# A two-layer block in one program: ScalarE takes the first layer norm of the dispatch stage, VectorE finds six of eight inverse roots from bits, and TensorE's order in a group is rearranged

## The reference, cut to what matters

```python
x = layernorm(x + attn(x))      # x: (4, 1024, 128) float32; attn ends in silu(y) @ W_out
x = layernorm(x + ffn(x))
# ffn: logits = flat @ router_w.T ; the 2 best of 8 experts, weights from a softmax
#      out  = sum over chosen experts e of mlp_e(flat) * weight + mlp_shared(flat)
#      mlp(x) = square(relu(x @ w_fc.T)) @ w_proj.T       d_ff = 512
# layernorm(x) = (x - mean) / sqrt(var + 1e-5), over the 128 features
```

## Time and profile before

| | |
|---|---|
| median of 3 runs | 514.8 us (514.63 to 515.39) |
| the profiled execution | 513.47 us; its span from first to last instruction is 511.6 us |
| TensorE busy in the span | 450.6 us (88%) |
| VectorE busy | 374.9 us (73%) |
| ScalarE busy | 357.7 us (70%) |
| GpSimd busy | 294.5 us (58%) |
| mean granted TensorE clock | 0.967 of full |

### The profile page before, as it was taken

One profiled execution on the slowest core, in us unless ns is written; L12 is line 12 of the kernel. 1 busy time (PEld: TensorE's weight loads), 2 busy tenths in 40 slices (PEclk: granted clock), 3 DMA queues, 4 the chain that ended last, 5 costly groups with the idle time before them and its releaser, 6 DMA issues.

```text
span 511.6 us, 7508 instructions
## 1 busy us (share of the span) xinstructions
PE 450.6 (88%) x2162; PEld 293.2 (57%) x2162; DVE 374.9 (73%) x863; ACT 357.7 (70%) x545; POOL 294.5 (58%) x250
## 2 busy tenths in 40 slices
PE   8757899998999988887888999689999999999391
PEld 5313344433443333344666777479999999999340
DVE  6776999998999999999998976533433334555075
ACT  3839799998999999971555566427666666566256
POOL 3235567777677787873767677714455555655200
PEclk9979999999999999999799999979999999999897
DMA  8010010109955566000111111131222221221373
GB/s 264 4 43 0 1 43 1 44 2 375 350 210 209 211 222 229 32 1 2 45 42 49 36 49 57 54 90 52 68 69 78 65 64 57 70 57 54 102 279 113
DMA packets 39448, 48.55 MB, mean 95 GB/s; under 512 B 5408, under 2 KB 25058, under 8 KB 38896
## 3 DMA queue, kind: packets, MB, share of 16 engines
q1 hardware_dynamic: 34048, 39.06, 22.7%
q0 software_dynamic: 5216, 8.70, 5.5%
q10 hardware_dynamic: 144, 0.31, 0.2%
HBM read 19.17 MB, written 29.11 MB: 94 GB/s over the span
## 4 chain that ended last, share of the span: by engine, by line
DVE 41%; PE 35%; ACT 8%; issue 7%; POOL 4%; DMA 3%; DVEq 0%; ACTq 0%; POOLq 0%; SPq 0%
PE routed_ph L1388 13%; PE routed_po L1401 12%; DVE memory_y_raw L735 10%; DVE memory_prod L726 10%; DVE memory_feat L711 4%; PE dispatch_spo L927 3%; POOL table_scratch L1080 3%; ACT finish_xo L1566 2%; PE memory_nsum L585 2%; DVE dispatch_xrow L1148 2%; PE dispatch_sph L917 2%; PE routed_px L1376 1%; DVE memory_query L706 1%; DMA memory_feat<-memory_last_rows 1%; ACT memory_feat L377 1%
## 5 line engine op out<-in xcount | busy, mean ns | idle before, releaser
L465 POOL TENSOR_TENSOR memory_feat<-memory_feat,memory_p_tok 128x1024 f32<-128x1024 f32 x64 | 121.5, 1920 | 54.7 <-ACT memory_feat L377 54.7
L585 PE MATMUL memory_nsum<-memory_feat,tri 128*128 128x512 f32 x256 | 116.5, 598 | 10.8 <-ACT memory_last_rows L386 4.3
L1364 POOL DMA_INDIRECT pick_scratch<-routed_ob,routed_xg x71 | 70.9, 998 | 74.3 <-DVE routed_ob L1485 60.8
L585 PEld LDWEIGHTS memory_nsum<-memory_feat,tri 128*128 128x128 f32 x256 | 46.9, 190 | 70.0 <-issue 66.7
L1080 POOL DMA_INDIRECT table_scratch<-dispatch_xrow,dispatch_slot x64 | 61.8, 966 | 27.7 <-issue 17.1
L1434 ACT ACTIVATE routed_rel<-routed_ph 128x512 f32<-128x512 f32 x71 | 42.3, 597 | 46.1 <-PE routed_ph L1388 46.1
L1388 PE MATMUL routed_ph<-routed_xs,routed_w1c 128*128 128x256 f32 (+1 forms) x368 | 71.3, 337 | 0.9 <-DVE routed_w2c L1471 0.9
L1485 DVE TENSOR_SCALAR routed_ob<-routed_po,routed_xg 128x128 f32<-128x128 f32 x71 | 22.6, 348 | 67.2 <-PE routed_po L1401 67.2
L1401 PE MATMUL routed_po<-routed_w2c,routed_hid 128*128 128x128 f32 x568 | 71.1, 275 | 0.5 <-ACT routed_hid L1443 0.5
L726 DVE TENSOR_TENSOR memory_prod<-memory_nsum,memory_query 128x1024 f32<-128x1024 f32 x58 | 68.2, 1215 | 1.9 <-PE memory_nsum L585 1.9
L1401 PEld LDWEIGHTS routed_po<-routed_w2c,routed_hid 128*128 128x128 f32 x568 | 67.0, 192 | 0.8 <-ACT routed_hid L1443 0.7
(11 more groups left out here) (187 smaller groups left out, 662.1 us busy)
## 6 DMA issues: line engine op xcount, KB each, us to landing
table_scratch<-memory_blank SPq DMA_DIRECT2D x68, 260.0 KB, 2.8
finish_pick<-pick_scratch SPq DMA_DIRECT2D x16, 256.0 KB, 5.6
routed_xg<-table_scratch SPq DMA_DIRECT2D x25, 130.0 KB, 2.2
x_tok<-x SPq DMA_DIRECT2D x4, 512.0 KB, 3.9
w<-w_up SPq DMA_DIRECT2D x2, 1024.0 KB, 9.0
w<-w_down SPq DMA_DIRECT2D x2, 1024.0 KB, 11.1
out<-finish_xo SPq DMA_DIRECT2D x8, 256.0 KB, 2.3
routed_xg<-table_scratch SPq DMA_DIRECT2D x21, 65.0 KB, 1.9
```

The lines of the kernel that those rows point to most:

```text
L465: last = nc.gpsimd.tensor_tensor(v, v, pv, ALU.mult)
L585: last = nc.tensor.matmul(nsum[:, o:o + 512], tri[:], feat[:, i % U, h, q * 512:(q + 1) * 512], start=True, stop=True)
L1364: nc.gpsimd.indirect_dma_start(out=pick_dram, in_=ob[:, u, h, :], in_offset=None, out_offset=bass.IndirectOffsetOnAxis(ap=xg[:, t % XU, h, ...
```

## The change

ScalarE does `normalise` as an Identity activation with a scale (the root) and a bias (`shift` = -mean times root, one more VectorE instruction). The root is found in `invert_root`: GpSimd's power for groups 0 and 1 alone, else from bits with three Newton steps. `res`, `scale`, `shift` are double buffered. In TensorE's loop `project` goes ahead of `turn_x`, `turn_x` behind `up(g, 0)`, `route` behind the first `down`, and `rank` or `total` behind the third `down`. ScalarE's list gets `normalise` in four places, and `keep_x` and `slope` move.

```diff
-POWERS = (0, 1, 2, 4, 6)
+POWERS = (0, 1)
+STEPS = 3
...
                 for g in range(1, NG):
-                    if g + 1 < NG:
-                        turn_x(g + 1)
                     if g + 2 < NG:
                         project(g + 2)
                     up(g, 0)
                     if g + 1 < NG:
+                        turn_x(g + 1)
+                    down(g - 1, 0)
+                    if g + 1 < NG:
                         route(g + 1)
-                    down(g - 1, 0)
                     up(g, 1)
                     down(g - 1, 1)
+                    up(g, 2)
+                    down(g - 1, 2)
                     if g + 1 < NG:
                         rank(g + 1)
                     else:
                         total()
-                    up(g, 2)
-                    down(g - 1, 2)
                     up(g, 3)
...
+            def normalise(g):
+                act.wait_ge(shift_done, g + 1)
+                for t in range(GT):
+                    last = nc.scalar.activation(xrow[:, 0, g * GT + t, 0:D], res[:, g % 2, t, :], ACT.Identity,
+                                                bias=shift[:, g % 2, t:t + 1], scale=scale[:, g % 2, t:t + 1])
+                last.then_inc(x1_done, 1)
...
                 if i == NT - 3:
+                    normalise(0)
                     for g in range(2, NG - 2):
                         silu(g)
                     nc.scalar.copy(tri_r[:], tri[:])
...
                 keep_x(0)
                 second_row(0)
                 slope(0)
+                normalise(1)
                 keep_y(2)
                 for g in range(NG):
-                    if 0 < g < NG - 1:
-                        keep_x(g + 1)
                     relu(g, 0)
                     square(g, 0)
                     if 0 < g < NG - 1:
+                        keep_x(g + 1)
                         second_row(g + 1)
                     relu(g, 1)
...
                     square(g, 1)
                     if g == 0:
                         second_row(1)
-                    if 0 < g < NG - 1:
-                        slope(g + 1)
+                    if g + 2 < NG:
+                        normalise(g + 2)
                     relu(g, 2)
                     square(g, 2)
-                    if g == 0:
-                        slope(1)
+                    if g < NG - 1:
+                        slope(g + 1)
...
-            def normalise(g):
+            def invert_root(g):
                 dve.wait_ge(var_done, g + 1)
+                if g >= 2:
+                    dve.wait_ge(x1_done, g - 1)
...
-                for n in range(1 if g in POWERS else 4):
+                steps = 1 if g in POWERS else STEPS
+                for n in range(steps):
...
-                for t in range(GT):
-                    last = nc.vector.tensor_scalar(xrow[:, 0, g * GT + t, 0:D], res[:, t, :], mv[:, t, 0:1],
-                                                   root[:, t:t + 1], ALU.subtract, ALU.mult)
-                last.then_inc(x1_done, 1)
+                nc.vector.scalar_tensor_tensor(shift[:, g % 2], mv[:, :, 0], -1.0, scale[:, g % 2], ALU.mult, ALU.mult
+                                               ).then_inc(shift_done, 1)
...
                     if g + 2 < NG:
                         residual(g + 2)
+                        invert_root(g + 2)
                     if g + 1 < NG:
                         choose(g + 1)
-                    if g + 2 < NG:
-                        normalise(g + 2)
```

More of the change, by code:

```diff
@@ L177, in __init__ @@
         self.newton = sb("newton", [P, 2, GT])
+        self.scale = sb("scale", [P, 2, GT])
+        self.shift = sb("shift", [P, 2, GT])
         self.off = sb("off", [P, E])
@@ L790, in dispatch @@
         stride, base0, past, owner, moved = early.stride, early.base0, early.past, early.owner, early.moved
-        bits = early.bits
+        bits, scale, shift = early.bits, early.scale, early.shift
         ones_r = sb("ones_r", [P, P], F32R)
@@ L813, in dispatch @@
         root_done = sem("root_done")
+        shift_done = sem("shift_done")
         x1_done = sem("x1_done")
@@ L1121, in residual @@
                 dve.wait_ge(proj_done, g + 1)
-                if g:
-                    dve.wait_ge(x1_done, g)
-                else:
+                if g >= 2:
+                    dve.wait_ge(x1_done, g - 1)
+                elif g == 0:
                     dve.wait_ge(mem.x_tok_in, 16 * B)
-                link(nc.vector.tensor_tensor(res[:].rearrange("p t c -> p (t c)"), pb[:],
+                link(nc.vector.tensor_tensor(res[:, g % 2].rearrange("p t c -> p (t c)"), pb[:],
                                              x_tok[:, group(g), :].rearrange("p t c -> p (t c)"), ALU.add))
                 for t in range(GT):
-                    last = nc.vector.bn_stats(stats[:, t, :], res[:, t, :])
+                    last = nc.vector.bn_stats(stats[:, t, :], res[:, g % 2, t, :])
                 link(last)
@@ L1142, in normalise @@
                     link(nc.vector.tensor_scalar(root[:].bitcast(I32), bits[:], -1.0, float(ROOT_SEED), ALU.mult, ALU.add))
-                for n in range(1 if g in POWERS else 4):
+                steps = 1 if g in POWERS else STEPS
+                for n in range(steps):
                     link(nc.vector.tensor_tensor(newton[:, 0], var[:], root[:], ALU.mult))
                     link(nc.vector.scalar_tensor_tensor(newton[:, 1], newton[:, 0], -0.5, root[:], ALU.mult, ALU.mult))
-                    link(nc.vector.scalar_tensor_tensor(root[:], newton[:, 1], 1.5, root[:], ALU.add, ALU.mult))
-                for t in range(GT):
-                    last = nc.vector.tensor_scalar(xrow[:, 0, g * GT + t, 0:D], res[:, t, :], mv[:, t, 0:1],
-                                                   root[:, t:t + 1], ALU.subtract, ALU.mult)
-                last.then_inc(x1_done, 1)
+                    link(nc.vector.scalar_tensor_tensor(root[:] if n + 1 < steps else scale[:, g % 2], newton[:, 1], 1.5,
+                                                        root[:], ALU.add, ALU.mult))
+                nc.vector.scalar_tensor_tensor(shift[:, g % 2], mv[:, :, 0], -1.0, scale[:, g % 2], ALU.mult, ALU.mult
+                                               ).then_inc(shift_done, 1)
             def choose(g):
@@ L1243, in tail @@
                 elif i == NT - 3:
-                    normalise(0)
+                    invert_root(0)
                 elif i == NT - 2:
@@ L1252, in rest @@
                 count(0)
-                normalise(1)
+                invert_root(1)
                 reduce(NT - 4)
```

4 lines of the change are left out of this document (3 added, 1 removed).

## The result

The changed kernel takes 529.6 us (median of 6 runs, 528.84 to 531.38), the kernel before in the same session 514.7 us (6 runs, 513.16 to 515.39): ratio 1.030, 95% interval 1.0276 to 1.0327. The change makes the kernel 3% slower. The direction was as predicted; 525.4 us and the range up to 528.0 were too low.

A forecast was written before the change was run, and what follows sets the result against it. TensorE's start of the first routed `up` was taken to bound the kernel; opening 7.3, loop 2.0, `total` 1.75, `down(7)` -0.5 sum to +10.6 us, 514.8 to 525.4 us, 8-in-10 range 519.5 to 528.

The forecast's parts named there:

- the half clock: TensorE's opening at 1.2 GHz: `project` 1.7, `route` 1.55, first half of the sums 2.7 for 1.8 us.
- the collision of `scale` with the next VectorE instruction: GpSimd's `scale` beside x1: moving x1 saves 1.4 us of VectorE time in two groups, left as slack.
- TensorE's own work in a group: Loop: one full group counted at 10.15 us from start to start.
- What bounds the kernel: Routed stage untouched; the first routed `up`, at 341.44, decides, and the end follows when TensorE reaches `total`.
- First stop: Opening: `normalise(0)` ahead of `keep_y(1)` on ScalarE; `project(1)` +3.2 us, `place(0)` +4.6 us.
- Second stop: Opening: `normalise(1)` ahead of `keep_y(2)` on ScalarE; `project(2)` +7.1 us, `up(1, 0)` +7.3 us.
- the third stop: `normalise(2)` ahead of `keep_y(3)` on ScalarE, which ends at 262.1; mentioned but not priced apart.
- The loop: From `up(1, 0)` to `up(7, 0)`: exposed hand-overs `keep_y` and `keep_x` make it 67.1 us for 65.1, +2.0.
- That VectorE's gain is slack: Loop: VectorE comes down to some 8.1 us a group, under TensorE's 10.15; the roots change nothing.
- The end: `total` moves behind an `up` and a `down`, +1.75 us; `down(7)` taken at 5.7 us, -0.5.
- Sum: All terms together +10.6 us; the median 514.8 becomes 525.4 us.
- Rival 4: Newton steps run into GpSimd's `scale`, or half clock returns in each group; up to +14 us, 528.8; chance 0.07.

The follow-up runs named there:

- e3: Changed kernel with `normalise(0)` moved behind `keep_y(1)` and `normalise(1)` behind `keep_y(2)`: 552.0 us, ratio 1.017, on a slower chip.
- e6: e12 with TensorE's loop order, the early ranks and total, and ScalarE's `keep_x` back as before, VectorE's order left as changed: 532.7 us, ratio 1.038.
- e12: The same kernel as e3, run again beside a steadier kernel before: 524.6 us, ratio 1.019.
- e14: e12 with `normalise(g+2)` behind `keep_y(g+3)`, `choose` ahead of the root, `total` at its old place, `keep_x` ahead of `relu(g, 0)`: 520.5 us, ratio 1.010.
- e5: The changed kernel run again without any edit: 530.3 us, ratio 1.030.
- e7: Kernel before with only the roots of groups 2 to 7 from bits, three Newton steps, no power on GpSimd for them: 515.4 us, ratio 1.003.
- e11: Changed kernel with one edit, `choose(g+1)` ahead of the root of group g+2 on VectorE: 550.4 us, ratio 1.071.
- e9: Changed kernel with `total()` alone back at its old place, ahead of `up(7, 2)` and `down(6, 2)`: 527.5 us, ratio 1.026.
- e13: Changed kernel with products whose values are overwritten, ten, twelve and eight ahead of `project(1)`, `project(2)`, `project(3)`: 528.0 us, ratio 1.027.
- e10: e6 with VectorE's order of before restored as well (residual, choose, root): 528.8 us, ratio 1.030.
- e17: Kernel before with `add_shared(6)` between the table's halves, group 6's root from bits, four unused products behind `down(7)`: 511.6 us, ratio 0.994.
- e8: Kernel before with one edit, `add_shared(6)` between the two halves of VectorE's table of tiles: 514.8 us, ratio 1.002.

## Why the prediction was right in direction and too low

The way and the path were right; the size was not. The steps that failed are three terms of the sum: the half clock (charged to 5 us of work at the first stop, it lasted some 10; with what followed from it 2.4 us in the opening, 0.5 in group 1 and 0.8 at the end), the collision of `scale` with the next VectorE instruction (put at nothing, 1.5 us), and TensorE's own work in a group (10.15 us for 10.55, 1.0 over the loop).

- **What bounds the kernel** held: the routed stage did not move, and the start of its first `up` carries the whole difference.
- **First stop**: said +4.6 at `place(0)`, measured 6.2 (249.53 less the 1.3 of the memory stage). The waiting was right to the tenth: `project(1)` +3.2. The term that was mis-sized is the half clock. I charged it to `project`, `route` and the first half of the sums; it lasted from 237 to 247 and all the sums took 6.16 us.
- **Second stop**: `project(2)` +8.65 for +7.1, by what the first had left behind. `up(1, 0)` +9.7 for **+7.3**: 6.2 in the first half of A, 3.5 in the second for 2.7. The path was right: with both stops away 7.9 of the 9.7 go where the clock stays up (e3, e6), 5.2 where it falls all the same (e12). I had the third stop, `normalise(2)` ahead of `keep_y(3)`, and the root ahead of `choose(1)` in the sum as a result of late `project(2)`, and did not see that they are late without it: with the first two stops away the second half is still 1.6 us above before, and e14, which moves those as well, takes another 4.6 off it.
- **The loop**: said +2.0, measured +5.0. Groups came out at 13.1, 12.3, 13.8, 11.7, 9.7 and 9.7 for 12.4, 12.1, 12.1, 11.5, 9.5 and 9.5. The waits for `keep_y` (0.49 and 1.01) and `keep_x` (0.49) were seen, and about right with the overlap of 0.15 us that the trace hides. Put at nothing were 1.5 us in group 3, the collision of `scale` with `sel`: I had counted `scale` as slack gained, since x1 would be out of its way. e5 shows that it is no accident. Group 1 had some 0.5 us more of half clock. The last 1.0 is 0.1 to 0.3 us in every group: TensorE's own work, counted at 10.15 us from start to start, is short. Group 4 of the kernel before, in which TensorE waits for nothing, lasts 10.55:

```profile
292.90:303.45 10.55, 10.45 (x71) 8.29 (x70) 6.91 (x43) 6.57 (x12) 8.34 (x9) 1.00 0.14 46
```

- **That VectorE's gain is slack**: right (e7), with one qualification by e6 and e11: VectorE's order is not slack. The changed kernel's late `rank` and its root ahead of `choose` belong together; each undone without the other makes it slower (e6, which undoes other orders too, and e11).
- **The end**: +1.75 for `total` was right in the trace. `down(7)` was to take 5.7 us and took 6.38, mostly on the lower clock; -0.5 became +0.3.
- **Sum**: 9.7 + 5.0 + 1.75 + 0.3 = 16.8 in this execution for 10.6, and 14.9 between the medians; the profiled execution was the slowest of its six. Rival 4 had two of the ingredients, the half clock and a collision, at a chance of 0.07; both were terms, not accidents. One reading behind it was wrong: the Newton instruction of 1.83 us did not run into `scale` but into GpSimd's product over `memory_feat`, which runs from 228.61 to 232.38; the instruction ends at 232.40.

What stays open: by the ratios e12, e9 and e13 give back 5.5, 2.2 and 1.3 us; they overlap (both stops and the clock), and how they add was not measured. Why the clock fell in e12 and not in e3, at the same kernel and the same wait, no run shows. Why B took 96 to 100 us on the first chip, against 75 here, stays open too: in e3's trace VectorE is idle 11.8 us in four pieces in front of its copy of the logits, put down to a releaser outside the core, and TensorE waits 2.2 to 3.2 us for `sel` in four groups.

## What to carry to other kernels

An instruction moved to an idle engine is priced by its place in that engine's list: first find the latest input it can wait for, then what stands behind it. If what stands behind it feeds that input, the wait grows with each turn. Undo orders in the pairs in which they were made, and when one chain is cut, look at once for the second, here less than 2 us behind.

## What the runs showed of the hardware

- GpSimd's product of 128x512, 1.11 us long, held up the VectorE instruction that it met: x1 (1.14 to 2.53 us, in the other group 2.68), `sel` (0.19 to 1.74), a cast (0.17 to 1.56), and Newton instructions (0.16 to between 1.63 and 1.80 in e10, e11 and e14). `sel` and the cast end 0.06 and 0.04 us after it. The Trainium skill, page "SBUF — State Buffer", section "Who interferes with whom", says that a VectorE instruction with two inputs in SBUF, like `sel`, meets GpSimd on the shared read port, and a cast or a tensor_scalar (x1) where it runs in a two-port mode; the rows agree, but for the mode, which they do not show. With x1 gone from VectorE the collision went to another instruction; where VectorE was idle, as beside the changed kernel's first `scale` (274.52), it held up nothing, and neither did it hold up an instruction with one of its inputs in PSUM (the first of `place`, 0.19 us beside it in e12, and 0.19 elsewhere).
- After waits of 2.11 and 2.29 us on TensorE in a lean stretch, the granted clock was at its lower level (1.2 GHz) from 237 to 247, and stayed there through 8 us of work without a gap (from 238.76). After the wait of 2.10 us alone it fell in e12 and not in e3, the same kernel. Products of no use in the gap held it up from 236 to 256 in e13, and at the end of dispatch in e17, where the first routed products took 3.62 us for 4.75 in e8.
- From the issue of GpSimd's last scatter to the first turn of gathered rows are 4.75 us in e8 (333.72 to 338.47) and 4.81 in e17 (334.14 to 338.95).
